# Decoder kernel: four of a head's 26 masked score pieces get their mask from VectorE instead of TensorE

## The chip, the cores and the metric

The kernel runs on one core of one Trainium2 chip. The metric is the device time of one execution in microseconds, as the median of several runs. TensorE does the matmuls (its weight loads have rows of their own, PEld), VectorE (DVE) and ScalarE (ACT) read and write both SBUF and PSUM, GpSimd (POOL) works in SBUF, and SyncE (SP) issues most DMAs.

## The reference

Two decoder layers run over 2048 tokens of width 256. Each has causal self-attention, cross-attention to a context of 1601 rows, and a feed-forward part. All attentions have 16 heads of 16 dimensions. The change touches only the cross-attention of the first layer, the one with an explicit mask:

```python
qh, kh, vh = (split_heads(qp), split_heads(kp), split_heads(vp))
scores = jnp.einsum('bhqd,bhkd->bhqk', qh, kh) / jnp.sqrt(jnp.float32(D_K))
scores = jnp.where(mask == 0, NEG_INF, scores)
attn = jax.nn.softmax(scores, axis=-1)
ctx = jnp.einsum('bhqk,bhkd->bhqd', attn, vh)
```

The mask has one value for each query and key (2048 x 1601), the same for all heads.

## The kernel before

All four attentions are one function, `attention_phase`; the flag `masked` is true only for the one that the change touches. A head's scores are computed twice.

**Units: the row maxima.** Softmax needs the maximum of every query row. A unit is 128 queries by 401 keys (or 398 at the end of a row): four matmuls on TensorE (line 548), then one instruction on VectorE that adds the mask in bfloat16 and takes the maximum (line 733, with a short row that reads the accumulator). A head has 16 x 4 = 64 units. Units go through three PSUM banks (`M_BANKS = 3`): TensorE fills unit g only after VectorE has finished unit g - 3, `pe.wait_ge(unit_used, g - M_BANKS + 1)`. `finish_max` (lines 745 to 758) turns a head's maxima into rows that are stacked under its queries, in five short VectorE steps that stand ahead of units 0 to 4 of the next head.

**Pieces: scores, mask, exponential, product.** Here the keys lie on the partitions. 13 tiles of up to 128 keys times two halves of 1024 queries make 26 pieces per head, numbered n = 0 to 25. The even pieces are the first halves. For a piece TensorE writes the scores (`scores`, line 569, eight matmuls, four column tiles in each of two PSUM banks), then adds the mask in PSUM (`mask_scores`, line 587, eight matmuls of -2^30 times the identity by a 0/1 mask in fp8, `mask_one`). ScalarE takes the exponential (line 475). After an odd piece, TensorE multiplies the tile by the values (`product`, line 609). Pieces use two PSUM buffers of two banks in turn, so the scores of piece n + 2 wait until the exponential of piece n is done.

**The order on TensorE** is written out by one loop, head by head and slot by slot. In slot n come: the scores of piece n + 2; the first units that are due here (the larger half of them); the mask products of piece n + 2; the product of the tile if n is odd; the other units. Each slot has two or three units, taken from the next head (slots 0 to 17, units 19 to 63) or from the head after that (slots 18 to 25, units 0 to 18). Slots 0|1 have 2 + 1 | 1 + 1 units (ahead of the mask products + behind them), slots 6|7 and 12|13 have 1 + 1 | 2 + 1, and slots 18|19 have 1 + 1 | 1 + 1.

**The order on VectorE** is simply unit after unit, head after head. Behind the last head's `finish_max` stand `scale(0)`, a copy, `invert(1)`, `scale(1)` and `invert_last`, which divide the heads' outputs by the sums of their exponentials (lines 789, 858, 784, 796). `invert(1)` and `scale(1)` have two DMAs between them, over which the inverse sums go to memory and come back (lines 302 and 309, on SP).

## Time and profile before

| what | value |
|---|---|
| runs (3) | 3050.74, 3052.56, 3059.14 us; median 3052.56 |
| profiled execution | 3052.74 us, of which the span is 3051.0 us |
| TensorE, busy share of the span | 92% |
| VectorE, busy share | 71% |
| ScalarE, busy share | 60% |
| mean granted TensorE clock | 0.952 of full speed |
| masked attention, from its first unit to its last unit on VectorE | 603.4 to 1269.5 us |
| its mask products on TensorE (line 587) | 3264 matmuls, from 645.8 to 1310.5 us |

A timeline row gives the start in the span, the time that the row took, the engine, the line, the operation with its tiles, a count, and in brackets how long the engine had stood idle and what released it. Matmuls are pipelined, so rows of TensorE overlap: four column tiles run at once, and a row of eight 512-column matmuls that lasts 0.62 us can have the next row start 0.44 us after it. The start-to-start distance is what to read.

### The profile page before, as it was taken

How to read it: one execution, taken by the hardware profiler on the slowest of the kernel's cores; microseconds unless marked ns; L12 is line 12 of the kernel's file. 1: busy time of each engine (PE TensorE's matmuls, PEld its weight loads, DVE VectorE, ACT ScalarE, POOL GpSimd, SP SyncE). 2: the span in 40 equal slices, each digit the busy share in tenths (PEclk: the TensorE clock that was granted, in tenths of full speed). 3: DMA queues.
4: the chain of work that ended last, by engine and by line, in shares of the span. 5: the costliest groups of instructions: out<-in, count | busy, mean ns of one | idle time of the engine just before them, and what ended most of it. 6: DMA issues, size and time to landing. Idle time of an engine off the chain costs nothing. (4 is left out here: it accounts for less than half of the span.)

```text
span 3051.0 us, 93944 instructions
## 1 busy us (share of the span) xinstructions
PE 2817.6 (92%) x39186; PEld 1046.2 (34%) x39187; DVE 2171.2 (71%) x6062; ACT 1824.3 (60%) x2158; POOL 542.7 (18%) x760
## 2 busy tenths in 40 slices
PE   4999999999999999967999998999999999899997
PEld 2522222522222222233222224652222222256664
DVE  7688986587878887565899993158888888652114
ACT  2388878436666666734588886234777777831222
POOL 0188870110000000001222113111000000002330
PEclk7899999979999999978899999997999999999999
DMA  3345541301110001102111112020111111111112
GB/s 98 111 130 131 135 111 35 118 18 25 25 26 25 17 24 26 36 20 76 33 47 43 42 45 83 1 74 23 39 52 52 52 53 32 35 58 62 44 43 86
DMA packets 120407, 166.79 MB, mean 55 GB/s; under 512 B 38227, under 2 KB 89310, under 8 KB 119984
## 3 DMA queue, kind: packets, MB, share of 16 engines
q1 hardware_dynamic: 102192, 117.21, 14.3%
q0 software_dynamic: 12320, 43.02, 4.6%
q8 instruction: 310, 5.08, 0.7%
q10 hardware_dynamic: 5472, 0.56, 0.2%
q14 instruction: 113, 0.93, 0.1%
HBM read 126.51 MB, written 26.72 MB: 50 GB/s over the span
## 5 line engine op out<-in xcount | busy, mean ns | idle before, releaser
L737 DVE TENSOR_REDUCE mpart<-ps 128x1 f32<-128x512 f32 (+2 forms) x1792 | 1014.2, 616 | 149.2 <-PE ps L548 148.1
L548 PE MATMUL ps<-stack 48*32 48x401 f16 (+5 forms) x13312 | 987.9, 355 | 55.3 <-DVE mpart L737 25.3
L475 ACT ACTIVATE xT<-ps,exp_scale 128x1024 f32<-128x1024 f32 (+3 forms) x800 | 794.6, 1028 | 284.6 <-PE ps L569 137.5
L475 ACT ACTIVATE cn<-ps,exp_scale 128x1024 f32<-128x1024 f32 (+4 forms) x800 | 743.1, 959 | 233.6 <-PE ps L569 119.7
L569 PE MATMUL ps<-stack 50*32 50x512 f16 (+3 forms) x11648 | 744.4, 377 | 56.2 <-ACT xT L475 42.3
L548 PEld LDWEIGHTS ps<-stack 48*32 48x32 f16 x13312 | 293.3, 91 | 1056.6 <-DVE mpart L737 562.8
L733 DVE CUSTOM_DVE_ANT_0 scrap<-ps,arena 128x401 bf16<-128x401 f32 (+1 forms) x1024 | 534.3, 574 | 128.0 <-PE ps L548 128.0
L609 PE MATMUL ps<-xT,vall 128*17 128x512 f32 (+4 forms) x3648 | 422.5, 524 | 2.2 <-POOL xT L434 1.4
L609 PE MATMUL ps<-cn,vall 128*17 128x512 f32 (+3 forms) x3392 | 412.9, 508 | 1.0 <-ACT cn L475 1.0
L569 PEld LDWEIGHTS ps<-stack 50*32 50x32 f16 x11648 | 194.6, 91 | 209.2 <-ACT xT L475 110.5
L727 DVE CUSTOM_DVE_ANT_0 scrap<-ps,scrap 128x128 bf16<-128x128 f32 (+3 forms) x512 | 247.6, 485 | 19.7 <-PE ps L548 15.1
L587 PE MATMUL ps<-arena,big 128*32 128x512 fp8e4 (+1 forms) x3264 | 256.8, 386 | 0.0
L1671 PE MATMUL ps<-arena,vall 128*128 x312 | 146.7, 593 | 0.6 <-ACT vall L1745 0.6
L1928 DVE TENSOR_TENSOR vall<-osb,ps 128x512 f32<-128x512 f32 x39 | 26.8, 688 | 146.0 <-PE ps L1671 146.0
L1761 ACT ACTIVATE osb<-ps 128x512 f32<-128x512 f32 x39 | 23.3, 597 | 169.8 <-PE ps L1671 169.8
L1152 POOL PARTITION_ALL_REDUCE small<-small x1 | 0.4, 371 | 687.4 <-issue 687.4
L609 PEld LDWEIGHTS ps<-xT,vall 128*17 128x17 f32 (+1 forms) x3648 | 71.5, 96 | 111.2 <-issue 46.1
L1574 POOL IOTA vall<- 128x16 f32 x1 | 0.2, 153 | 608.1 <-POOLq L248 608.1
L609 PEld LDWEIGHTS ps<-cn,vall 128*17 128x17 f32 (+1 forms) x3392 | 70.5, 96 | 109.0 <-issue 54.6
L422 POOL TENSOR_SCALAR arena<-wbuf 128x401 bf16<-128x401 int32 x64 | 101.2, 1581 | 6.3 <-DMA wbuf<-in_mask 2.5
L587 PEld LDWEIGHTS ps<-arena,big 128*32 128x32 bf16 (+1 forms) x3264 | 50.3, 94 | 120.8 <-issue 120.8
L733 DVE DVE_READ_ACCUMULATOR2_ANT mpart<- 128x1 f32 x1024 | 84.7, 83 | 0.0
(281 smaller groups left out, 2510.9 us busy)
## 6 DMA issues: line engine op xcount, KB each, us to landing
stack<-q_parts SPq DMA_DIRECT2D x384, 64.0 KB, 2.6
stack<-k_parts SPq DMA_DIRECT2D x192, 64.0 KB, 2.9
wbuf<-in_maskT POOLq DMA_DIRECT2D x24, 512.0 KB, 4.7
arena<-in_moe_w SPq DMA_DIRECT2D x19, 512.0 KB, 4.4
stack<-k_parts SPq DMA_DIRECT2D x192, 50.0 KB, 2.3
stack<-sums_inverse SPq DMA_DIRECT2D x16, 512.0 KB, 5.6
parts<-osb SPq DMA_DIRECT2D x240, 32.0 KB
wbuf<-in_mask POOLq DMA_DIRECT2D x16, 401.0 KB, 4.0
```

The source lines that it names most:

```text
L422: chain.link(nc.gpsimd.tensor_scalar(e.mask_add[:, t, a:a + n], stage.bitcast(I32), 0.0, MASKED, ALU.is_equal, ALU.mult))
L475: nc.scalar.activation(e.prob[tile % P_SLOTS][0:rows, half * HALF + first:(half + 1) * HALF], S_PS(g)[0:rows, first:HALF], ACT.Exp, scale= ...
L548: last = nc.tensor.matmul(bank[quarter(j), 0:w], qs[b][rows, t * P + 32 * j:t * P + 32 * j + 32], ks[b][rows, a:a + w], start=True, stop=True)
L569: last = nc.tensor.matmul(S_PS(g)[quarter(j), lo:hi], ks[b][at:at + KM, kt * P + 32 * j:kt * P + 32 * j + 32], qs[b][at:at + KM, half * HA ...
L587: last = nc.tensor.matmul(S_PS(g)[quarter(j), lo:hi], e.big16[0:rows, quarter(j)], e.mask_one[0:rows, kt, half * HALF + lo:half * HALF + h ...
L609: last = nc.tensor.matmul(O_PS[quarter(j, HD + 1), b0 * P:CH], e.values[0:rows, kt, h, :], weights[0:rows, b0:4, j, :], start=(kt == 0), s ...
L727: nc.vector.tensor_tensor_reduce(out=e.scrap[:, t % 3, 0:w], in0=src, in1=e.scrap[:, 3, CH - w:CH], scale=1.0, scalar=-3.0e38, op0=ALU.add ...
L733: nc.vector.tensor_tensor_reduce(out=e.scrap[:, g % 4, 0:w], in0=src, in1=e.mask_add[:, t, a:a + w], scale=1.0, scalar=-3.0e38, op0=ALU.ad ...
L737: nc.vector.tensor_reduce(dst, src, AX, ALU.max).then_inc(unit_used, 1)
L1671: last = nc.tensor.matmul(bank, e.pair_xT[i % 2][:, c, :], w, start=(c == 0), stop=(c == NC - 1))
L1761: nc.scalar.activation(e.gated_s[i % 2], a_bank(i), ACT.Silu).then_inc(pair_silu, 1)
L1928: nc.vector.tensor_tensor(e.pair_h[i % 2], e.gated_s[i % 2], b_bank(i), ALU.mult).then_inc(pair_h, 1)
```

## The change

For pieces 2, 8, 14 and 20 of each head, `mask_scores` returns at once, and `scores` counts up a new semaphore, `scored`. VectorE waits for it and does the masking itself: one `scalar_tensor_tensor` over 128 x 1024 elements that reads the scores in PSUM and the fp8 mask in SBUF and writes the sum back to the same PSUM. ScalarE's exponential of such a piece waits for this instruction (`piece_masked`). Waits on `s_ready` are counted in 22 pieces per head instead of 26. All pieces concerned are even ones with full 128-key tiles. On VectorE the instruction for piece n stands directly ahead of the first unit of slot n - 2. The last pieces, for which no unit is left (piece 20 of head 14 and all four of head 15), stand together behind the last `finish_max`, ahead of `scale(0)`.

```diff
+        by_dve = (2, 8, 14, 20) if masked else ()
+        own = [n for n in range(ns) if n not in by_dve]
+        scored, piece_masked = (sem("scored"), sem("piece_masked")) if masked else (None, None)
...
-                        act.wait_ge(s_ready, g + 1)
+                        if n in by_dve:
+                            act.wait_ge(piece_masked, h * len(by_dve) + by_dve.index(n) + 1)
+                        else:
+                            act.wait_ge(s_ready, h * len(own) + own.index(n) + 1)
...
-                    if not masked:
+                    if n in by_dve:
+                        last.then_inc(scored, 1)
+                    elif not masked:
                         last.then_inc(s_ready, 1)
...
                     kt, rows, half, first, diagonal, _ = slots[n]
+                    if n in by_dve:
+                        return
...
+                def mask_piece(h, i):
+
+                    n = by_dve[i]
+                    kt, rows, half, _, _, _ = slots[n]
+                    dve.wait_ge(scored, h * len(by_dve) + i + 1)
+                    nc.vector.scalar_tensor_tensor(out=S_PS(h * ns + n)[0:rows], in0=e.mask_one[0:rows, kt, half * HALF:(half + 1) * HALF],
+                                                   scalar=MASKED, in1=S_PS(h * ns + n)[0:rows], op0=ALU.mult, op1=ALU.add).then_inc(piece_masked, 1)
+
+                def unit_of_step(h, u):
+
+                    for i, n in enumerate(by_dve):
+                        ahead = 1 if n - 2 <= turn else 2
+                        if h - ahead >= 0 and before[n - 2] == u:
+                            mask_piece(h - ahead, i)
+                    unit(h, u)
...
-                        unit(h, u)
+                        unit_of_step(h, u)
...
                 for step in range(MAX_STEPS):
                     finish_max(H - 1, step)
+                for h in range(H - 2, H):
+                    for i, n in enumerate(by_dve):
+                        if h + (1 if n - 2 <= turn else 2) >= H:
+                            mask_piece(h, i)
                 scale(0)
```

How the rows move. First TensorE, slots 6 and 7 of head 0. L569 (L575 in the changed file) are scores, L548 (L554) units, four matmuls each, L587 (L597) mask products, L609 (L619) the product. Before:

```order
L569 MATMUL ps<-stack_13216 32x512 x8
L548 MATMUL ps<-stack_13216 32x401 x4
L587 MATMUL ps<-arena,big 32x512 x8
L548 MATMUL ps<-stack_13216 32x398 x4
L569 MATMUL ps<-stack_13216 32x512 x8
L548 MATMUL ps<-stack_13216 32x401 x8
L587 MATMUL ps<-arena,big 32x512 x8
L609 MATMUL ps<-cn,vall 17x512 x4
```

And now:

```order
L575 MATMUL ps<-stack_13216 32x512 x8
L554 MATMUL ps<-stack_13216 32x401 x4
L554 MATMUL ps<-stack_13216 32x398 x4
L575 MATMUL ps<-stack_13216 32x512 x8
L554 MATMUL ps<-stack_13216 32x401 x8
L597 MATMUL ps<-arena,big 32x512 x8
L619 MATMUL ps<-cn,vall 17x512 x4
```

The mask products of piece 8, between the two units of slot 6, are gone. Everything else keeps its order.

VectorE at the same place. The rows named ISA are units of L733 (now L743), each followed by the row that reads its accumulator; the rows begin with the last unit of slot 5. Before:

```order
L733 ISA scrap,mpart<-ps,arena 128x401
L733 ISA mpart 128x1
L733 ISA scrap,mpart<-ps,arena 128x401
L733 ISA mpart 128x1
L733 ISA scrap,mpart<-ps,arena 128x398
```

And now:

```order
L743 ISA scrap,mpart<-ps,arena 128x401
L743 ISA mpart 128x1
L754 SCALAR_TENSOR_TENSOR ps<-arena,ps 128x1024
L743 ISA scrap,mpart<-ps,arena 128x401
L743 ISA mpart 128x1
L743 ISA scrap,mpart<-ps,arena 128x398
```

The masking of piece 8 stands between the last unit of slot 5 and the first of slot 6.

VectorE at the end of the attention, behind the last unit of head 15 (L789 are `scale(0)` and `scale(1)`, L784 is `invert(1)`). Before:

```order
L745 TENSOR_REDUCE mfin<-mpart 128x16
L749 TENSOR_SCALAR mrest<-mfin 128x16
L751 TENSOR_SCALAR mneg<-mrest 128x16
L753 SCALAR_TENSOR_TENSOR mneg<-mneg,mrest 128x16
L758 STREAM_TRANSPOSE mturn<-mneg 128x32
L789 TENSOR_TENSOR parts<-parts,stack_13216 128x1024 x2
L858 COPY parts<-ident 128x128
L784 RECIPROCAL parts<-parts 128x128
L789 TENSOR_TENSOR parts<-parts,stack_13216 128x1024 x2
```

And now:

```order
L784 STREAM_TRANSPOSE mturn<-mneg 128x32
L754 SCALAR_TENSOR_TENSOR ps<-arena,ps 128x1024 x5
L815 TENSOR_TENSOR parts<-parts,stack_13216 128x1024 x2
L888 COPY parts<-ident 128x128
L810 RECIPROCAL parts<-parts 128x128
L815 TENSOR_TENSOR parts<-parts,stack_13216 128x1024 x2
```

Five maskings (head 14's piece 20 and head 15's four) stand ahead of `scale(0)` and `invert(1)`.

## Rows read from the trace of the kernel before

**Rows 1.** Windows: a stretch of the masked attention (columns as named)

```profile
core 0: us, PE busy (x) PEld busy (x) DVE busy (x) ACT busy (x) POOL busy (x), PEclk, DMA share, GB/s
900.00:1000.00 100.00, 99.30 (x1816) 26.83 (x1808) 79.60 (x313) 69.43 (x65) 0.00 (x0) 1.00 0.11 27
```

**Rows 2.** Timeline of slots 6 and 7 of a middle head

```profile
1038.04 0.56 PE L569 MATMUL ps<-stack 50*32 50x512 f16 x8
1038.43 0.58 DVE L733 CUSTOM_DVE_ANT_0 scrap<-ps,arena 128x401 bf16<-128x401 f32 x1 [0.66 <-PE ps L548]
1038.54 0.62 PE L587 MATMUL ps<-arena,big 128*32 128x512 fp8e4 x8
1038.93 0.57 DVE L733 CUSTOM_DVE_ANT_0 scrap<-ps,arena 128x401 bf16<-128x401 f32 x1
1039.08 0.35 PE L548 MATMUL ps<-stack 48*32 48x398 f16 x4
1039.43 0.08 DVE L733 DVE_READ_ACCUMULATOR2_ANT mpart<- 128x1 f32 x1
1039.57 0.10 PEld L548 LDWEIGHTS ps<-stack 48*32 48x32 f16 x4 [0.35 <-DVE mpart L733]
1039.85 0.62 PE L587 MATMUL ps<-arena,big 128*32 128x512 fp8e4 x8
```

**Rows 3.** Timeline of slots 0 and 1 of the same head

```profile
1028.79 0.57 DVE L733 CUSTOM_DVE_ANT_0 scrap<-ps,arena 128x398 bf16<-128x398 f32 x1
1029.68 0.41 PE L569 MATMUL ps<-stack 50*32 50x512 f16 x8 [0.23 <-ACT xT L475]
1029.91 0.34 PE L548 MATMUL ps<-stack 48*32 48x401 f16 x4
```

**Rows 4.** Timeline of slots 18 and 19, where a head's units end

```profile
1016.16 0.22 DVE L745 TENSOR_REDUCE mfin<-mpart 128x16 f32<-128x64 f32 x1
1016.30 0.57 DVE L733 CUSTOM_DVE_ANT_0 scrap<-ps,arena 128x401 bf16<-128x401 f32 x1
1016.33 2.17 ACT L475 ACTIVATE cn<-ps,exp_scale 128x1024 f32<-128x1024 f32 x2 [0.80 <-PE ps L587]
1018.13 0.55 PE L569 MATMUL ps<-stack 50*32 50x512 f16 x8
```

**Rows 5.** Lines by form, VectorE: what 1024, 512 and 2048 elements take

```profile
L1033 DVE SCALAR_TENSOR_TENSOR wbuf<-vall,wbuf 128x1024 f32<-128x1024 f32 x1 | 1.2, 1226 | 0.0
L714 DVE SCALAR_TENSOR_TENSOR parts<-ps,bcol,parts 128x512 f16<-128x512 f32 x44 | 33.0, 751 | 54.2 <-ACT parts L455 54.2
L1068 DVE TENSOR_TENSOR turning<-ps,vall 128x2048 f32<-128x2048 f32 x4 | 9.2, 2292 | 0.1
```

**Rows 6.** Timeline of the end: heads 14 and 15, then the division

```profile
1269.77 2.12 ACT L475 ACTIVATE xT<-ps,exp_scale 128x1024 f32<-128x1024 f32 x2 [0.78 <-PE ps L587]
1270.64 2.32 DVE L789 TENSOR_TENSOR parts<-parts,stack 128x1024 f32<-128x1024 f32 x2
1271.39 0.41 PE L569 MATMUL ps<-stack 50*32 50x512 f16 x8
1286.44 0.95 DVE L784 RECIPROCAL parts<-parts 128x128 f32<-128x128 f32 x1 [13.35 <-DMA parts<-sums]
1296.65 2.36 DVE L789 TENSOR_TENSOR parts<-parts,stack 128x1024 f32<-128x1024 f32 x2 [9.26 <-DMA stack<-sums_inverse]
1303.82 0.41 PE L569 MATMUL ps<-stack 50*32 50x512 f16 x8
1316.10 0.96 DVE L796 RECIPROCAL osb<-ps 128x128 f32<-128x128 f32 x1 [17.08 <-PE ps L685]
```

**Rows 7.** The unmasked cross-attention: a window, then three starts of `finish_max`

```profile
2200.00:2210.00 10.00, 9.30 (x124) 1.76 (x116) 6.42 (x13) 5.96 (x7) 0.00 (x0) 0.66 0.27 64
...
2188.21 0.22 DVE L745 TENSOR_REDUCE mfin<-mpart 128x16 f32<-128x64 f32 x1
2226.92 0.22 DVE L745 TENSOR_REDUCE mfin<-mpart 128x16 f32<-128x64 f32 x1
2263.28 0.22 DVE L745 TENSOR_REDUCE mfin<-mpart 128x16 f32<-128x64 f32 x1
```

More of the change, by code:

```diff
@@ L256, in load @@
                     if h >= 3:
-                        sp.wait_ge(s_ready, (h - 2) * ns)
+                        sp.wait_ge(s_ready, (h - 2) * len(own))
                     for row, (k_part, q_part) in zip(range(0, KQ, HD), ((0, 0), (0, 1), (1, 0))):
@@ L305, in load_inverse @@
                     sp.wait_ge(rec_out, 16 * (c + 1))
-                    sp.wait_ge(s_ready, (14 + c) * ns)
+                    sp.wait_ge(s_ready, (14 + c) * len(own))
                     for a in range(0, S, HALF):
@@ L570, in scores @@
                                                     qs[b][at:at + KM, half * HALF + lo:half * HALF + hi],
-                                                    start=True, stop=not (crossed or masked))
+                                                    start=True, stop=not (crossed or masked and n not in by_dve))
                         if crossed:
```

## The prediction, made before the changed kernel was run

> **What bounds the kernel now.** I read the page's busy shares and the 40 slices first: the masked attention is the stretch where TensorE is fullest. A window says it exactly: in 100 us TensorE is busy for 99.3, VectorE for 79.6, ScalarE for 69.4, at a granted clock of 1.00 [rows 1]. So TensorE is the bound, and shares alone would welcome the change: it takes work from the full engine and gives it to one that is idle a fifth of the time.
>
> Shares don't say when the idle time comes, so I read the timeline of two slots [rows 2]. VectorE's idle time is one piece, 0.66 us, in front of the unit that TensorE fills right behind the product. During mask products and product TensorE fills no unit, and VectorE runs dry. Elsewhere the two are tied: the second unit of slot 7 (weights at 1039.57, 0.35 idle, released by VectorE) starts as soon as the bank that it needs is read. That bank held the first unit of slot 6, whose VectorE row starts at 1038.93 and whose accumulator row ends at 1039.43 + 0.08 = 1039.51; 0.06 later TensorE goes on. The mask products of piece 9 follow at 1039.85, and the product behind them.
>
> **What the change removes.** A group of mask products (8 matmuls) starts at 1038.54 and the next unit at 1039.08 [rows 2]: 0.54 us. There are 4 x 16 = 64 such groups, so at most 64 x 0.54 = 34.6 us.
>
> **What it adds.** 64 instructions on VectorE. The trace has none that reads and writes PSUM, or that reads fp8. Nearest: the same operation with an immediate scalar on 1024 fp32 elements in SBUF, 1.226 us; with a PSUM input, 512 elements take 0.751. From 512 to 2048 elements it costs (2.292 - 0.751)/1536 = 1.00 ns each, so 1024 with PSUM come to 0.751 + 0.51 = 1.26 [rows 5]. What counts behind it is the distance to the next start, which I call P. Two 1024-element rows together take 2.32 us [rows 6], so the second starts about 1.10 after the first; a unit of 0.58 has its follower 0.50 later [rows 2]. I take P = 1.14, with ends at 1.10 and 1.29 (nothing overlapped, some slack). The duration, for ScalarE's start, is 1.22 to 1.29.
>
> A page states another distance. The Trainium skill, VectorE: DVE Perf Modes, "The DRAIN you can't avoid", says that "the next op does not start until the 8-stage pipe empties", though the section behind it lets an instruction that isn't held start earlier. The rows of this trace agree with the second, by the overlaps just named. By the first the sum below would be some 7 us higher.
>
> **Pieces 8 and 14 (slots 6|7, 12|13).** VectorE takes its instructions in order: last unit of slot 5, masking, first unit of slot 6. The scores are there in time (from 1038.04, for 0.56, while the unit ahead lasts until 1038.93) [rows 2]. The masking starts at 1038.93, the first unit of slot 6 P later, its bank is free P later, and the second unit of slot 7 starts at 1039.57 + P. TensorE is in order too: piece 9's mask products and the product stand behind that unit. The 0.54 saved lies ahead of this wait and is swallowed by it. Before, TensorE waited there already, so the whole of P is paid: 1.14. Then come mask products and product without a new unit; VectorE, which ran dry there for 0.66 us before, works off its full banks and is dry again when the next unit comes, so the next pair of slots runs at the old pace. Nothing is given back, since nothing else there has slack. ScalarE ends the late exponential 1.1 us after the masking, well ahead of the scores two slots on.
>
> **Piece 2 (slots 0|1).** Here TensorE before stood waiting for ScalarE (1029.68), and the first unit of slot 1 starts at 1029.91 [rows 3]. Slot 0's first unit, on VectorE at 1028.79, now starts P later, at 1029.93, and frees its bank at 1029.93 + 0.50 + 0.08 + 0.06 = 1030.57. Cost 0.66, that is P - 0.48.
>
> **Piece 20 (slots 18|19).** The unit that needs the late bank stands behind the product, so there the units cost nothing. But ScalarE is late: the masking follows `mfin` at 1016.30 and is ready by 1017.55, the exponential that began at 1016.33 runs from 1017.6 to 1018.7, and the scores two slots on, at 1018.13 before, wait for it until 1018.8 [rows 4]. A further 0.1 goes to the units behind. Cost 0.75.
>
> Pieces 2, 8 and 14 occur so in heads 0 to 14: 15 x (0.66 + 2 x 1.14) = 44.1 us. Piece 20 in heads 0 to 13: 14 x 0.75 = 10.5.
>
> **The end.** Head 14's piece 20 is masked behind the five steps, from 1270.6 (where `scale(0)` stood) to 1271.9; its exponential and the next end near 1273.1 and 1274.1, and the scores that started at 1271.39 wait: 1.8 us. Head 15 has no units. A piece's own chain (scores 0.41, masking 1.25, exponential 1.06) is longer than the slots by about 0.5: 4 x 0.5 = 2.0. Then the division. Piece 20's scores came at 1303.82, so its masking ends near 1305.5, and behind it stand `scale(0)` 2.3, the copy 0.2 and the reciprocal 0.95: 1309.0 instead of 1287.4. From there to `scale(1)` it is two DMAs on SP's queue, 9.26 us, then 2.36: 1320.6. `invert_last` began at 1316.10 and needs VectorE [rows 6]. TensorE's totals and the last head's DMAs wait for it: 4.5 us.
>
> **Sum.** 44.1 + 10.5 + 1.8 + 2.0 + 4.5 = 62.9. On the profiled execution (3052.74, span 3051.0 and 1.7 around it) that gives 3115.6; the median of the runs is 0.2 lower, 3115.5. I say 3116. With P = 1.10 the 45 terms with P are 1.8 us less, with 1.29 they are 6.8 more, and the end may be off by 3 either way: 3111 to 3126 for this case. Edits that cost nothing: the counts of `s_ready` (the pieces that SP and the stacks wait for are masked by TensorE as before), and the five steps of `finish_max`, up to 0.9 us later, whose rows reach the stack over a microsecond ahead of the first scores that read them, which are late by as much.
>
> **Rivals.**
>
> *The clock falls as well.* Each stall leaves TensorE idle for about 1.2 us, and for a little more just ahead of it. In the unmasked attention, which has no mask products, the granted clock falls in some heads: 0.66 of full speed between 2200 and 2210, that is partly at 1.2 GHz. A head with such a fall takes 2226.92 - 2188.21 = 38.71 us, one without 2263.28 - 2226.92 = 36.36: 2.35 us more [rows 7]. Against it: the second of these heads has no fall, and in the masked stretch the clock stands at 1.00 [rows 1]. One fall per head gives 16 x 2.35 = 38, so 3153. The Trainium skill, TensorE: Matmul & The Clock Gate, "A second HAM failure mode: psum-queue depth-cycling", tells of the same mechanism: short idle times between groups of matmuls that cycle through banks make the clock oscillate. Chance 0.23.
>
> *The saved products count after all.* If the units behind a masking are not tied as tightly as rows 2 show, and TensorE takes its 0.54 off each wait, pieces 8 and 14 cost 0.60 and piece 2 0.12: 15 x 1.32 = 20, with the other terms (18.8) 39, so 3092. Against it: the wait at 1039.57 has no slack. Chance 0.10.
>
> *The masking is dear.* In place in PSUM, with fp8, it might take twice the time, as no row excludes: P = 2.3, 45 x 1.16 = 52 more, and piece 20 and the end 20 more: 3188. Chance 0.06.
>
> *VectorE absorbs it: faster.* Three pairs of slots hold 3 x 0.66 = 2.0 us of VectorE's idle time, more than P, and a masking comes only every three or four pairs. If TensorE weren't held at the second unit behind a masking, it would keep most of 34.6 us and lose only the 8 at the end: 3052.6 - 34.6 + 8 = 3026. It decides at the unit of 1039.57: its bank would have to be free more than 1.14 us ahead of TensorE's wish, and by rows 2 it is just free. Chance 0.04, with 0.02 that gain and loss cancel to within 0.3% (about 9 us, which is what a measurement of this kernel tells from no change).
>
> **How the numbers follow.** The case of the sum has 0.55. Faster 0.04, same 0.02, slower 0.94. The range reaches from the third case's side, 3090, to one fall of the clock in each head and a little more, 3160; outside are the dear masking and the gain.
>
> **What would show it.** The new rows: 64, of 1.2 to 1.3 us, each followed by a unit about 1.14 later; mask products 2752 instead of 3264. In slots 7 and 13 TensorE's weights for the second unit should stand idle for about 1.5 us, released by VectorE, and heads should lie 3.7 us farther apart. VectorE's share in the masked stretch should rise, TensorE's fall to some 90%. In the end `scale(1)` should come just ahead of `invert_last`. The forecast is wrong if the second unit of slots 7 and 13 doesn't wait, or if the clock leaves 1.00 in the masked stretch.

## The result, and the profile after

The changed kernel takes 3131.97 us (median of 4 runs, 3129.27 to 3134.27) against 3055.85 (4 runs, 3050.74 to 3060.33): a ratio of 1.0249, with a 95% interval of 1.0227 to 1.0271. It is slower, by 76 us. The forecast was 3116, with a range of 3090 to 3160.

The window that answers to [rows 1], with the columns of that group:

```profile
900.00:1000.00 100.00, 89.84 (x1582) 24.64 (x1575) 82.10 (x294) 62.80 (x58) 0.00 (x0) 0.98 0.08 20
```

TensorE went from 99.3 to 89.8 busy, by more than the mask products that it gave up (nine groups of 0.54 at most in such a stretch), and VectorE rose only to 82.1. No engine is full now. The granted clock is 0.98 where it was 1.00.

The timeline of slots 6 and 7, which answers to [rows 2]:

```profile
1079.15 0.35 PE L554 MATMUL ps<-stack 48*32 48x401 f16 x4
1080.06 1.23 DVE L754 SCALAR_TENSOR_TENSOR ps<-arena,ps 128x1024 f32<-128x1024 fp8e4 x1
1080.20 0.35 PE L554 MATMUL ps<-stack 48*32 48x401 f16 x4
1081.19 0.57 DVE L743 CUSTOM_DVE_ANT_0 scrap<-ps,arena 128x401 bf16<-128x401 f32 x1
1081.82 0.10 PEld L554 LDWEIGHTS ps<-stack 48*32 48x32 f16 x4 [1.53 <-DVE mpart L743]
1081.83 0.35 PE L554 MATMUL ps<-stack 48*32 48x401 f16 x4 [1.28 <-DVE mpart L743]
1082.11 0.61 PE L597 MATMUL ps<-arena,big 128*32 128x512 fp8e4 x8
1082.55 1.63 PE L619 MATMUL ps<-xT,vall 128*17 128x512 f32 x8
```

The masking starts at 1080.06 and the next unit 1.13 later. TensorE has issued the first unit of slot 7 (1080.20) and its second one stands until 1081.82, released by VectorE; matmuls are idle for 1.28. From the last unit of slot 5, which opens the pair here (1079.15), to the mask products of piece 9 (1082.11) are 2.96 us; before they were 1.83 (1038.02 below to 1039.85 in [rows 2]). The last row shows a fall of the clock: eight matmuls of the product last 1.63 us instead of 1.03.

How much each pair of slots pays is read from the starts of the product's weights, one set in each odd slot, in the weight loads of the timeline. The kernel before (its row of L548 is the last unit of slot 5, just ahead of slots 6 and 7):

```profile
1016.94 0.32 PEld L609 LDWEIGHTS ps<-xT,vall 128*17 128x17 f32 x8
1020.25 0.32 PEld L609 LDWEIGHTS ps<-cn,vall 128*17 128x17 f32 x8
...
1026.71 0.33 PEld L609 LDWEIGHTS ps<-xT,vall 65*17 65x17 f32 x8
1030.41 0.32 PEld L609 LDWEIGHTS ps<-xT,vall 128*17 128x17 f32 x8
1033.63 0.32 PEld L609 LDWEIGHTS ps<-cn,vall 128*17 128x17 f32 x8
...
1038.02 0.10 PEld L548 LDWEIGHTS ps<-stack 48*32 48x32 f16 x4 [0.85 <-DVE mpart L733]
...
1056.19 0.32 PEld L609 LDWEIGHTS ps<-xT,vall 128*17 128x17 f32 x8
1059.16 0.33 PEld L609 LDWEIGHTS ps<-cn,vall 128*17 128x17 f32 x8
```

The changed kernel:

```profile
1010.81 0.32 PEld L619 LDWEIGHTS ps<-xT,vall 128*17 128x17 f32 x8
1015.00 0.32 PEld L619 LDWEIGHTS ps<-xT,vall 128*17 128x17 f32 x8
...
1021.45 0.33 PEld L619 LDWEIGHTS ps<-cn,vall 65*17 65x17 f32 x8
1025.80 0.32 PEld L619 LDWEIGHTS ps<-xT,vall 128*17 128x17 f32 x8
1029.02 0.32 PEld L619 LDWEIGHTS ps<-xT,vall 128*17 128x17 f32 x8
1032.24 0.32 PEld L619 LDWEIGHTS ps<-cn,vall 128*17 128x17 f32 x8
1036.60 0.32 PEld L619 LDWEIGHTS ps<-cn,vall 128*17 128x17 f32 x8
...
1053.83 0.32 PEld L619 LDWEIGHTS ps<-xT,vall 128*17 128x17 f32 x8
1056.56 0.32 PEld L619 LDWEIGHTS ps<-xT,vall 128*17 128x17 f32 x8
```

A pair without a masking takes 3.22 (1025.80 to 1029.02), as before (1030.41 to 1033.63). The pair with piece 8 takes 4.36 (1032.24 to 1036.60), 1.14 more, and piece 14's 4.35, 1.13 more. Piece 2's pair takes 4.35 (1021.45 to 1025.80) against 3.70, 0.65 more. Piece 20 first gains 0.24 (2.73 instead of 2.97 in the last pair shown), then loses 0.88 (1010.81 to 1015.00 is 4.19 instead of 3.31): 0.64. Together 3.56 per head.

The first steps of `finish_max` show the whole head, three of fifteen:

```profile
1010.28 0.22 DVE L771 TENSOR_REDUCE mfin<-mpart 128x16 f32<-128x64 f32 x1
1056.03 0.22 DVE L771 TENSOR_REDUCE mfin<-mpart 128x16 f32<-128x64 f32 x1
1103.21 0.22 DVE L771 TENSOR_REDUCE mfin<-mpart 128x16 f32<-128x64 f32 x1
```

The head between the first two takes 45.75, 3.5 more than the 42.21 of before; the next takes 47.18, and so do nine more of the fourteen. They hold one fall of the clock each, at 1.44 us. An eleventh lies in head 0: the second of the sixteen first steps comes 4.39 us later than before (682.85 against 678.46), and 2.92 of this are maskings.

Slots 18 and 19, answering to [rows 4], and then the end, answering to [rows 6]:

```profile
1056.16 1.22 DVE L754 SCALAR_TENSOR_TENSOR ps<-arena,ps 128x1024 f32<-128x1024 fp8e4 x1
1057.41 2.12 ACT L481 ACTIVATE cn<-ps,exp_scale 128x1024 f32<-128x1024 f32 x2 [2.03 <-DVE ps L754]
1058.58 0.41 PE L575 MATMUL ps<-stack 50*32 50x512 f16 x8 [0.31 <-ACT cn L481]
...
1378.19 1.23 DVE L754 SCALAR_TENSOR_TENSOR ps<-arena,ps 128x1024 f32<-128x1024 fp8e4 x1 [7.06 <-PE ps L575]
1379.33 2.35 DVE L815 TENSOR_TENSOR parts<-parts,stack 128x1024 f32<-128x1024 f32 x2
1391.11 2.36 DVE L815 TENSOR_TENSOR parts<-parts,stack 128x1024 f32<-128x1024 f32 x2 [8.43 <-DMA stack<-sums_inverse]
1393.38 0.95 DVE L822 RECIPROCAL osb<-ps 128x128 f32<-128x128 f32 x1
...
1395.88 0.58 SPq L248 DMA_DIRECT2D parts<-osb  x1
```

The masking of the last head's piece 20 is followed by the whole division, and `scale(1)` at 1391.11 stands just ahead of `invert_last` (1393.38), where before it had been done for 17 us. From the last head's first step (1337.91) to the `place_last` transfers (1395.88) it is 57.97 us; before it was 48.97.

Not all of these 9.0 us are the maskings' own. The window of this stretch in the changed kernel, and the same stretch of e5, an experiment below with the same five maskings:

```profile
1337.91:1395.88 57.97, 51.28 (x602) 15.20 (x594) 14.96 (x21) 36.79 (x36) 0.00 (x0) 0.94 0.09 25
```

```profile
1339.48:1394.50 55.02, 50.27 (x638) 15.47 (x634) 14.96 (x21) 36.62 (x36) 0.00 (x0) 1.00 0.10 26
```

The changed kernel has two more falls of the clock here (the windows 1342.30 to 1345.70 and 1352.50 to 1355.90 stand at 0.50 of full speed, 1.2 GHz), behind stalls in which TensorE waits for ScalarE. Where the end has no fall it takes 55.02 (e5) or 55.06 (e10, below), 6.1 more than before. So 6.1 are maskings and 2.9 are falls, and between the first of the first steps and `place_last` this trace holds thirteen falls.

From those transfers to the end of the span, both kernels take the same (1732.3 and 1732.4 us). The whole difference of the spans, 77.2, lies in the masked attention:

| term | measured, us | forecast |
|---|---|---|
| pieces 2, 8, 14: 15 heads x 2.92 | 43.8 | 44.1 |
| piece 20: 14 heads x 0.61 to 0.64 | 8.6 | 10.5 |
| the end, without its falls | 6.1 | 8.3 |
| 13 falls of the clock: 11 x 1.44, and 2.9 in the end | 18.7 | 0 |

### The profile page after: what moved, and what is told of

Read it like the earlier page. It is cut to its first block and busy times, and to the rows that moved or that the text cites. A ratio compares the mean times of both kernels' runs of the same rounds, so it can differ in the third digit from the quotient of the medians.

```text
span 3128.2 us, 92985 instructions
## 1 busy us (share of the span) xinstructions
PE 2828.4 (90%) x38675; PEld 1051.8 (34%) x38675; DVE 2239.6 (72%) x6126; ACT 1825.0 (58%) x2158; POOL 545.8 (17%) x760
## 5 line engine op out<-in xcount | busy, mean ns | idle before, releaser
L554 PE MATMUL ps<-stack 48*32 48x401 f16 (+5 forms) x13312 | 994.2, 356 | 109.8 <-DVE mpart L743 49.9
L575 PE MATMUL ps<-stack 50*32 50x512 f16 (+3 forms) x11648 | 739.6, 379 | 68.6 <-ACT xT L481 48.5
L554 PEld LDWEIGHTS ps<-stack 48*32 48x32 f16 x13312 | 295.7, 91 | 1124.9 <-DVE mpart L747 562.2
L743 DVE CUSTOM_DVE_ANT_0 scrap<-ps,arena 128x401 bf16<-128x401 f32 (+1 forms) x1024 | 534.9, 573 | 130.7 <-PE ps L554 130.7
L619 PE MATMUL ps<-xT,vall 128*17 128x512 f32 (+4 forms) x3648 | 427.9, 530 | 2.6 <-POOL xT L437 1.8
L619 PE MATMUL ps<-cn,vall 128*17 128x512 f32 (+3 forms) x3392 | 414.2, 510 | 1.1 <-ACT cn L481 1.0
L575 PEld LDWEIGHTS ps<-stack 50*32 50x32 f16 x11648 | 194.2, 90 | 234.3 <-ACT xT L481 120.3
L597 PE MATMUL ps<-arena,big 128*32 128x512 fp8e4 (+1 forms) x2752 | 222.8, 395 | 0.0
L619 PEld LDWEIGHTS ps<-xT,vall 128*17 128x17 f32 (+1 forms) x3648 | 71.5, 96 | 111.0 <-issue 47.8
L619 PEld LDWEIGHTS ps<-cn,vall 128*17 128x17 f32 (+1 forms) x3392 | 70.4, 96 | 108.8 <-issue 55.4
L754 DVE SCALAR_TENSOR_TENSOR ps<-arena,ps 128x1024 f32<-128x1024 fp8e4 x64 | 78.3, 1223 | 37.0 <-PE ps L575 37.0
L743 DVE DVE_READ_ACCUMULATOR2_ANT mpart<- 128x1 f32 x1024 | 84.2, 82 | 0.0
```

Of the source, the lines that this page charges most:

```text
L554: last = nc.tensor.matmul(bank[quarter(j), 0:w], qs[b][rows, t * P + 32 * j:t * P + 32 * j + 32], ks[b][rows, a:a + w], start=True, stop=True)
L575: last = nc.tensor.matmul(S_PS(g)[quarter(j), lo:hi], ks[b][at:at + KM, kt * P + 32 * j:kt * P + 32 * j + 32], qs[b][at:at + KM, half * HA ...
L597: last = nc.tensor.matmul(S_PS(g)[quarter(j), lo:hi], e.big16[0:rows, quarter(j)], e.mask_one[0:rows, kt, half * HALF + lo:half * HALF + h ...
L619: last = nc.tensor.matmul(O_PS[quarter(j, HD + 1), b0 * P:CH], e.values[0:rows, kt, h, :], weights[0:rows, b0:4, j, :], start=(kt == 0), s ...
L743: nc.vector.tensor_tensor_reduce(out=e.scrap[:, g % 4, 0:w], in0=src, in1=e.mask_add[:, t, a:a + w], scale=1.0, scalar=-3.0e38, op0=ALU.ad ...
L754: nc.vector.scalar_tensor_tensor(out=S_PS(h * ns + n)[0:rows], in0=e.mask_one[0:rows, kt, half * HALF:(half + 1) * HALF], scalar=MASKED, i ...
```

## The experiments

The table gives all twelve. "Head" is the distance of first steps without a fall of the clock, "falls" the number of the 14 distances that are longer by 1.4 us or more (in the changed kernel this leaves out the fall in head 0 and the two in the end; in e7 two of the distances hold two falls), "end" the time from the last head's first step to `place_last`. The ratio is to the kernel before.

| run | head, us | falls | end, us | median, us | ratio, 95% interval |
|---|---|---|---|---|---|
| before | 42.21 | 0 | 48.97 | 3052.26 to 3055.85 | |
| changed | 45.75 | 10 | 57.97 | 3131.97 | 1.0227 to 1.0271 |
| e1 products left out only | 41.95 | 0 | 48.96 | 3050.53 | 0.9975 to 1.0005 |
| e2 VectorE's work only | 45.75 | 0 | 48.97 | 3105.17 | 1.0153 to 1.0187 |
| e3 odd pieces | 43.73 | 0 | 54.81 | 3081.65 | 1.0071 to 1.0105 |
| e4 piece 8 only | 43.34 | 9 | 49.38 | 3086.64 | 1.0088 to 1.0122 |
| e5 filled | 45.74 | 10 | 55.02 | 3131.42 | 1.0238 to 1.0277 |
| e6 other order in slots 7, 13 | 44.24 | 1 | 56.34 | 3095.86 | 1.0119 to 1.0155 |
| e7 end on TensorE | 45.74 | 11 | 48.98 | 3120.65 | 1.0191 to 1.0229 |
| e9 pieces 8, 14, 20 | 45.09 | 6 | 56.87 | 3116.13 | 1.0186 to 1.0216 |
| e10 the same, filled | 45.09 | 0 | 55.06 | 3100.54 | 1.0137 to 1.0166 |
| e8 320 columns of 9 odd pieces | 41.19 | 0 | 49.01 | 3040.67 | 0.9933 to 0.9964 |
| e11 384 columns | 41.13 | 0 | 49.11 | 3035.11 | 0.9932 to 0.9961 |
| e12 480 columns | 41.31 | 0 | 49.14 | 3037.48 | 0.9928 to 0.9957 |

### The saving without the work, and the work without the saving

e1 leaves the four pieces unmasked:

```diff
                 def mask_piece(h, i):
 
                     n = by_dve[i]
                     kt, rows, half, _, _, _ = slots[n]
-                    dve.wait_ge(scored, h * len(by_dve) + i + 1)
+                    return
...
-                            act.wait_ge(piece_masked, h * len(by_dve) + by_dve.index(n) + 1)
+                            act.wait_ge(scored, h * len(by_dve) + by_dve.index(n) + 1)
```

> The changed kernel with the 64 VectorE instructions left out and nothing in their place: pieces 2, 8, 14 and 20 of each head get no mask at all (ScalarE waits for their scores alone). TensorE so does 64 x 0.54 = 34.6 us less than in the kernel before, and VectorE no more. Theory A (the second unit of slots 7 and 13 is tied to VectorE's read, so whatever TensorE saves ahead of it is swallowed): nothing at pieces 8 and 14, at most 0.5 per head at pieces 2 and 20, so 3048 to 3056 us, and in the trace the weights of that second unit stand idle for about 0.9 us, released by VectorE (0.35 before). Rival B (TensorE is the bound and what it saves counts): 3056 - 34.6 = 3021 us.

Measured: 3050.53, no difference from before. 34.6 us of matmuls are gone and nothing comes of it. The timeline of its slots 6 and 7 shows why:

```profile
1035.60 0.35 PE L554 MATMUL ps<-stack 48*32 48x401 f16 x4
...
1036.64 0.10 PEld L554 LDWEIGHTS ps<-stack 48*32 48x32 f16 x4 [0.50 <-DVE mpart L743]
1037.13 0.10 PEld L554 LDWEIGHTS ps<-stack 48*32 48x32 f16 x4 [0.40 <-DVE mpart L743]
1037.41 0.12 PEld L597 LDWEIGHTS ps<-arena,big 128*32 128x32 bf16 x8 [0.18 <-issue]
```

Both units of slot 7 wait for VectorE, which paces them. From the opening unit to piece 9's mask products it is 1.81 us (1035.60 to 1037.41), with 0.54 less to do than before, when it was 1.83. The weights stood for 0.40 to 0.50, not for 0.9: the waiting time was spread over two units. Only piece 20's saving of 0.25 stays, the 0.26 by which a head is shorter.

e2 keeps all mask products and gives VectorE the same instruction, from and to SBUF, at the same places:

```diff
+                    dve.wait_ge(spared, len(added_so_far) + 1)
+                    added_so_far.append(n)
+                    nc.vector.scalar_tensor_tensor(out=e.scrap[0:rows, 3, :].bitcast(FP8), in0=e.mask_one[0:rows, kt, half * HALF:(half + 1) * HALF],
+                                                   scalar=0.0, in1=e.vall[0:rows, 0:4, :].rearrange("p t c -> p (t c)"), op0=ALU.mult, op1=ALU.add, saturate=False).then_inc(spared, 1)
...
-                        unit(h, u)
+                        unit_of_step(h, u)
```

The instruction's result goes to the fourth quarter of `scrap`, so the units take turns in three quarters instead of four.

> The kernel before, with all its mask products, and on VectorE the same instruction form (fp8 mask, fp32 second operand, 128x1024) at the places of pieces 2, 8, 14 and 20, but from and to SBUF, with nobody waiting for its result; none behind the last head's steps, 59 in all. Theory A (the stall is VectorE's time ahead of a tied bank, the saved products are swallowed): heads become longer by 0.66 + 2 x 1.14 = 2.9 us (44 in all, piece 20's 0.75 was ScalarE's wait and goes, the end too), and the clock falls as in the changed kernel (about 1.4 us in each of 11 or 12 heads): 3055 + 44 + 16 = 3115 us. Rival B (the changed kernel was longer by VectorE's work less the products saved): it would be slower than the changed kernel less its end and its ScalarE wait: 3132 - 20 + 34.6 = 3147 us.

Measured: 3105.17, heads 45.75 apart, exactly as in the changed kernel without a fall. So what a head pays is VectorE's time, and the saved products count for nothing: shown from both sides. Two points of the expectation fell. The clock never fell, though the pairs with maskings took 4.36 as in the changed kernel. And piece 20 costs the same 0.63 although ScalarE waits for nobody:

```profile
1043.44 1.21 DVE L750 SCALAR_TENSOR_TENSOR scrap<-arena,vall 128x1024 fp8e4<-128x1024 fp8e4 x1
...
1046.35 0.35 PE L551 MATMUL ps<-stack 48*32 48x401 f16 x4 [0.22 <-DVE mpart L736]
```

Behind the steps of `finish_max` VectorE has its units and the steps to do with no idle time between, so the units there are tied as well.

### One slot later

e3 changes one line:

```diff
-        by_dve = (2, 8, 14, 20) if masked else ()
+        by_dve = (3, 9, 15, 21) if masked else ()
```

> Pieces 3, 9, 15 and 21 are masked by VectorE instead of 2, 8, 14 and 20: the same work on both engines, one slot later, so that the masking stands ahead of the first unit of the slot that ends in the product. Then VectorE's idle time of 0.66 us behind that slot takes part of it, and TensorE's saved 0.54 lies behind the tied unit. Theory A (the place costs, not the work): a piece costs 1.14 - 0.66 = about 0.5, in 15 heads x 4 pieces 28, the end 8 as before, stalls too short for the clock to fall: 3055 + 36 = 3091 us, 3080 to 3100. Rival (the cost is that of 64 instructions wherever they stand): 3132 us, as the changed kernel. Rival C (ScalarE becomes late, since the exponential of an odd piece has less time before the scores two slots on): over 3132.

Measured: 3081.65. The same 64 instructions cost 1.52 per head instead of 3.54. By the starts of the product's weights, read as above, piece 9's two pairs take 3.00 and 3.89 instead of twice 3.22, 0.45 more, piece 15's 0.47, piece 21's 0.63, and piece 3's nothing (6.91 instead of 6.92). The clock stays at 1.00 in all heads. The place makes more than half of the price.

e6 leaves the pieces as they are, but lets TensorE issue one unit instead of two ahead of the product in slots 7 and 13:

```diff
-                        middle = -(-len(now) // 2)
+                        middle = 1 if masked and n in (7, 13) else -(-len(now) // 2)
```

> The changed kernel, but in slots 7 and 13 TensorE issues one unit instead of two ahead of mask products and product, and two behind it. So the unit that has to wait for VectorE's late read is behind the product, and nothing is held up. Theory A (TensorE's order turns VectorE's lateness into a stall): pieces 8 and 14 cost about 1.14 - 0.66 = 0.5 each instead of 1.14, since VectorE no longer runs dry behind the masking; heads 44.4 to 44.5 us apart instead of 45.75, fewer clock falls; the end as in the changed kernel: 3055 + 15 x 2.25 + 9 = 3098 us without falls, 3112 with as many as before. Rival (the cost is VectorE's time, and order doesn't matter): 3132.

Measured: 3095.86, 36 us back by the order of a few matmuls, with the same work on every engine: 15 x 1.51 = 23 from shorter heads, and in the profiled executions eleven falls fewer (one in the heads and one in the end instead of thirteen), about 16. That adds up to 39; the 3 us too many are within what runs of one kernel differ. TensorE now does mask products and product while VectorE masks:

```profile
1009.47 1.22 DVE L754 SCALAR_TENSOR_TENSOR ps<-arena,ps 128x1024 f32<-128x1024 fp8e4 x1
1009.89 0.61 PE L597 MATMUL ps<-arena,big 128*32 128x512 fp8e4 x8
1010.33 1.03 PE L619 MATMUL ps<-cn,vall 128*17 128x512 f32 x8
```

Neither engine stands still until the product ends. Pieces 8 and 14 cost (44.24 - 42.21 - 0.65 - 0.64)/2 = 0.37 each.

### One piece, and the clock

e4 is the same line with `by_dve = (8,)`.

> VectorE masks piece 8 alone, TensorE the other 25. Theory A: one stall of P = 1.14 us in each of 15 heads, 17 us, half a microsecond in the last head, nothing at the division, since that masking comes before the middle of the last head: 3055 + 17.6 = 3073 us if a single stall per head leaves the clock alone. Theory D (any stall of this size makes the clock fall): 1.4 more per head, 3094 us. If pieces add up only by their number, a quarter of the changed kernel's +77: 3075, with heads of 42.21 + 1.24; by theory A alone heads lie 43.35 us apart, 1.14 more than the kernel before's 42.21.

Measured: 3086.64. Heads without a fall are 43.34 apart, 1.13 more, which is P to a hundredth. Nine of the fourteen hold a fall and are 1.5 longer. So both theories were half right: one stall of 1.28 us per head is enough for the clock to fall, in most heads but not in all.

In e2 pieces 2, 8 and 14 make the pairs just as long, and the clock never fell. What differs is the mask products, and with them the length of the stall: where they are kept they fill part of the gap, and TensorE's matmuls stand for 1.04 (piece 8) and 1.01 us (piece 14) in e2, against 1.28 in the changed kernel. e5 puts as many matmuls in their place, with zero weights, added to the output bank (the zero weights lie in the fourth quarter of `scrap`, so the units use three):

```diff
                     if n in by_dve:
+                        if n > 2:
+                            for bank in range(2):
+                                for j in range(-(-rows // 32)):
+                                    at = half * HALF + bank * CH
+                                    nc.tensor.matmul(O_PS[quarter(j, HD + 1), 0:CH], e.scrap[0:rows, 3, 0:HD + 1],
+                                                     e.mask_one[0:rows, kt, at:at + CH], start=False, stop=False)
                         return
```

> The changed kernel, and in the place of the mask products that it left out TensorE does as many of the same width with zero weights (pieces 8, 14 and 20; piece 2 not), added to the output bank, so that nothing is changed by them. The other three kernels of this kind so far: products kept beside the stalls (heads all 45.75 us apart, no clock fall) and products gone (47.2 in 10 of 14 heads). Theory E (the clock falls because TensorE does less around a stall, since 8 groups of matmuls are gone ahead of it): with this filling the falls go or become few, heads lie 45.75 apart, and the kernel with 1.5 us of work more per head is faster than the changed kernel: 3132 - 15 = 3117 us. Rival F (the stall alone makes the clock fall): as the changed kernel, 3132, or slower by up to 48 x 0.54 = 26 us if the filling isn't swallowed.

Measured: 3131.42, as the changed kernel, with falls still there. 48 groups more make no head longer (45.74), which shows once more that they are swallowed. By its time alone theory E fell. The profiled execution has ten falls instead of thirteen, but the clock also stands at half speed for longer at the opening of the attention (until 656.1 us instead of 649.4), which makes the first distance about 2.9 us longer; e7 shows the same without any filling. The windows show more: where the falls are now. First e5, whose head begins at 729.40, then the changed kernel, whose head begins at 728.59 (piece 2's stall comes 13 us into the head, piece 8's 25):

```profile
740.00:745.00 5.00, 3.84 (x76) 1.15 (x68) 4.34 (x14) 3.67 (x4) 0.00 (x0) 0.98 0.34 99
745.00:750.00 5.00, 5.00 (x72) 1.18 (x68) 3.02 (x13) 2.07 (x3) 0.00 (x0) 0.67 0.19 42
...
755.00:760.00 5.00, 3.96 (x84) 1.01 (x80) 4.34 (x16) 2.59 (x3) 0.00 (x0) 1.00 0.01 3
```

```profile
750.00:755.00 5.00, 3.64 (x76) 1.21 (x68) 4.34 (x14) 3.18 (x3) 0.00 (x0) 1.00 0.00 0
755.00:760.00 5.00, 5.00 (x72) 1.01 (x67) 2.77 (x11) 2.23 (x3) 0.00 (x0) 0.66 0.01 3
```

In e5 the clock falls behind piece 2's stall, the one without filling, and holds at 1.00 behind piece 8's, where TensorE was idle for 1.04 of 5 us instead of 1.36. The expectation of e10 below calls the filled stalls "as long"; they are not, they last 1.04 and 1.01 instead of 1.28. All ten falls of that trace lie 15 to 16 us into their head, behind piece 2. So e9 and e10 leave piece 2 to TensorE, `by_dve = (8, 14, 20)`, e9 without the filling, e10 with it.

> The changed kernel with piece 2 masked by TensorE again; VectorE masks 8, 14 and 20. Heads without a clock fall: 42.21 + 2 x 1.13 + 0.64 = 45.1 us apart. Theory E (the clock falls behind a stall where mask products were left out) and rival F (the stall alone does it) both give falls of 1.4 to 1.5 us in many heads: 3055 + 15 x 2.9 + 8 for the end + about 14 for ten falls = 3120 us; without falls 3107.

> The run before this one, and in the place of the left-out mask products of pieces 8, 14 and 20 TensorE does as many of the same width with zero weights, added to the output bank. In the first kernel with this filling every fall that was left came behind piece 2's stall, the one without filling, though the stalls of 8 and 14 were as long. Theory E: no falls at all here, all heads 45.1 us apart, 3107 us, some 14 below its neighbour, with more work on TensorE. Rival F (the stall alone): falls as in its neighbour, the same time. Rival G (the falls move to another place in the head): heads 46.5 us apart in most cases, the same time.

Measured: 3116.13 and 3100.54. The heads without a fall are the same, 45.09, and e10 has no fall in any head nor in the end. More matmuls, less time. The windows at the same stall (piece 14's), e9 first:

```profile
715.00:720.00 5.00, 3.64 (x60) 0.90 (x53) 3.69 (x11) 2.47 (x3) 0.00 (x0) 0.86 0.01 2
```

```profile
710.00:715.00 5.00, 3.99 (x68) 0.83 (x60) 4.22 (x15) 2.88 (x3) 0.00 (x0) 1.00 0.01 2
```

And e10's second unit at that stall, which in e9 stands for 1.28:

```profile
713.39 0.35 PE L555 MATMUL ps<-stack 48*32 48x401 f16 x4 [1.01 <-DVE mpart L752]
```

So filling the gap takes these falls away. It does so in two ways at once, more work ahead of the stall and a shorter stall, and no run takes the two apart. Nor does the length of a stall decide alone: in the end of e5 stalls of 1.59 and 1.39 us are followed by no fall, while the same wait of 1.39 for ScalarE is followed by one in the end of the changed kernel and of e1 (where VectorE masks nothing), and by none in e6. Behind piece 2, TensorE is idle for 0.30, 0.41 and 0.45 us in e5 as in e6, and the clock falls there in ten of fourteen heads of e5 and in one of e6. What singles out a head or a stall stays open.

Of the 15.6 us between the medians the two profiled executions explain 10.5 by the clock: six falls in the heads (8.7) and one in the end (1.8). They differ by another 4.1 ahead of the attention's first unit and by 5 behind its end, where the kernels are the same; that is what runs differ by, and not the filling.

### The end

e7 gives the five maskings that have no unit behind them back to TensorE:

```diff
+        def dve_masks(h, n):
+            return n in by_dve and h + (1 if n - 2 <= turn else 2) < H
...
-                    if n in by_dve:
+                    if dve_masks(h, n):
                         return
...
-                for h in range(H - 2, H):
-                    for i, n in enumerate(by_dve):
-                        if h + (1 if n - 2 <= turn else 2) >= H:
-                            mask_piece(h, i)
```

> The changed kernel, but the five maskings that stood behind the last head's steps (piece 20 of head 14, pieces 2, 8, 14 and 20 of head 15) are TensorE's products again. The time from the last head's first step to the place_last transfers was 48.97 us before and 57.97 after. Theory: the 9.0 us are the last head's longer chain (1.8 + 2.0) and the division behind the maskings (4.5); all of it goes back to 49, so 3132 - 9 = 3123 us. Rival (the end is late because the last exponentials are): less than 4 us come back.

Measured: 3120.65, and the end takes 48.98, as before, at a clock of 1.00. All of the 9.0 comes back, the 6.1 of the maskings and the 2.9 of the two falls, and the difference of medians, 11.3, is near it. The expectation added the 9.0 up as 1.8 + 2.0 + 4.5, without the falls. The heads keep theirs: the profiled execution has thirteen in eleven of the fourteen distances (two distances are 48.63), and at 3129.14 it is the slowest of this kernel's four.

### A version that uses VectorE's idle time

The runs say where the change could pay: VectorE is idle only behind the product's slot (0.66 us per pair), and a saving of TensorE counts only there. e8 starts from the kernel before; VectorE masks the last 320 columns of pieces 3, 5, ... 19 of heads 0 to 14, behind TensorE's mask products for the others:

```diff
+        by_dve, WIDE = tuple(range(3, 20, 2)) if masked else (), 320
...
-                        lo, hi = bank * CH, (bank + 1) * CH
+                        lo, hi = bank * CH, (bank + 1) * CH - (WIDE if bank and dve_masks(h, n) else 0)
...
+                    dve.wait_ge(s_ready, h * ns + n + 1)
+                    part = S_PS(h * ns + n)[0:rows, HALF - WIDE:]
+                    nc.vector.scalar_tensor_tensor(out=part, in0=e.mask_one[0:rows, kt, (half + 1) * HALF - WIDE:(half + 1) * HALF],
+                                                   scalar=MASKED, in1=part, op0=ALU.mult, op1=ALU.add).then_inc(piece_masked, 1)
...
+                    for i, n in enumerate(by_dve):
+                        if before[n - 2] + 1 == u:
+                            mask_part(h - 1, i)
                     unit(h, u)
```

> The kernel before, with VectorE masking the last 320 of the 1024 columns of pieces 3, 5, ... 19 of heads 0 to 14, each ahead of the second unit of the slot two ahead (which ends in the product), and TensorE the other 704. VectorE's part is some 0.1 + 0.32 = 0.43 us and fits its idle time of 0.66; TensorE saves 4 x 320 of its columns, 0.17 us, behind the tied unit, where the removal isn't swallowed. Theory A (idle time of VectorE is only to be had behind the product, and savings of TensorE only count there): eight or nine pairs of slots per head go from 3.22 to about 3.06 us, 15 x 8.5 x 0.16 = 20 us, so 3032 us, faster than both kernels. Rival (ScalarE or the second unit's bank ties the pair, and savings vanish as in the run with products left out): 3053. Rival (the masking delays as in the changed kernel): 9 x 0.43 x 15 = 58 us more, 3110.

e11 and e12 set `WIDE` to 384 and 480.

> As the kernel with 320 columns on VectorE, with 384. There a pair of slots took 3.09 us (TensorE 99.5% busy, VectorE 91%), and one masking 0.41 to the next start. With 384 it takes 0.47: VectorE needs 2.57 + 0.47 = 3.04 per pair, TensorE about 3.22 - 0.16 = 3.06. So TensorE is still the bound by a little, heads 41.0 us apart instead of 41.19, 3 us less in all: 3037. Rival (ScalarE's start, which waits for the masking, becomes the tie): heads over 41.2.

> The same with 480 columns: VectorE would need 2.57 + 0.57 = 3.14 us per pair, TensorE 3.03. Theory A (beyond about 390 columns VectorE's idle time is used up and it paces the pair): pairs of 3.14, heads 42.21 - 9 x 0.08 = 41.5, 3044 us, slower than with 384 columns and still a little faster than the kernel before. Rival (what TensorE saves goes on counting): heads 40.7, 3032.

Measured: 3040.67, 3035.11 and 3037.48, all three faster than the kernel before by 0.5%, and not to be told from each other by their intervals. The window of e11 and VectorE's rows of e12:

```profile
900.00:1000.00 100.00, 99.25 (x1877) 27.83 (x1876) 92.61 (x346) 71.41 (x67) 0.00 (x0) 1.00 0.10 24
```

```profile
1033.05 0.66 DVE L753 SCALAR_TENSOR_TENSOR ps<-arena,ps 128x480 f32<-128x480 fp8e4 x1
1033.62 0.57 DVE L741 CUSTOM_DVE_ANT_0 scrap<-ps,arena 128x401 bf16<-128x401 f32 x1
...
1036.12 0.66 DVE L753 SCALAR_TENSOR_TENSOR ps<-arena,ps 128x480 f32<-128x480 fp8e4 x1
```

A pair takes 3.09 us with 320 columns, 3.06 with 384 and 3.07 with 480 (1033.05 to 1036.12). With 480, VectorE never runs dry in these pairs: masking 0.57 and five units of 0.50. The expectation of 3.14 counted the units at 2.57 in all, 0.07 too much. So up to 384 columns TensorE is the bound, from there VectorE. With 320 columns a pair gained 0.13 instead of 0.16 and a head 1.02 instead of 1.36, which makes 15 x 0.34 = 5 of the 9 us by which e8 fell short of its 3032; the rest is within what its runs differ (3033.37 to 3044.86).

## Why the prediction was right, and what was missing

The time, 3131.97, lies in the stated range of 3090 to 3160, but outside the 3111 to 3126 of the case that the sum describes. The range held it because it had been stretched for a fall of the clock. By the forecast's own sign (it is wrong "if the clock leaves 1.00 in the masked stretch") its main case fell on this point, while the direction, the tied bank and the price per masking held.

*Nature of the bound.* Right. Slots 6 and 7 behave as [rows 2] said: the second unit of slot 7 stands 1.53 us, released by VectorE, and the pair is longer by 1.14 and 1.13, the P of the forecast.

*The saved products.* Right, and now shown: leaving them out gains nothing (e1), keeping them costs nothing (e2), and filling their place costs nothing (e5). The rival that they count after all is excluded, and so are the ones by which VectorE absorbs the maskings or the instruction is dear (64 rows of 1.223 us).

*P.* 1.14 was taken, 1.13 measured, with a duration of 1.22. The Trainium skill, VectorE: DVE Perf Modes, "The DRAIN you can't avoid", has the next operation wait until the pipe is empty, and adds that one that is not held starts earlier. The unit behind a masking starts 0.09 to 0.10 before the masking's row ends (1080.06 + 1.23 against 1081.19): these rows agree with the addition and not with the first statement, as the prediction had it.

*Piece 2.* 0.66 forecast, 0.65 measured.

*Piece 20.* 0.75 forecast, 0.64 measured: a loss of 0.88 less a gain of 0.24 that the forecast hadn't. Its mechanism was only half right. ScalarE's wait is there (0.31 at 1058.58), but "the unit that needs the late bank stands behind the product, so there the units cost nothing" was wrong: e2, without ScalarE's wait, loses as much through the units. The two delays lie side by side.

*The end.* 8.3 forecast, 9.0 measured, and removed by e7. That the two agree is luck: 2.9 of the 9.0 are two falls of the clock, and what the forecast meant comes to 6.1. Its two parts, the delay of the last pieces and the division, were each too high by about 1.1. In e5, whose end has no fall, the last masking starts 37.26 us behind the last head's first step, where the scores before were ready at 34.60: 2.7 of delay instead of 1.8 + 2.0. From there to `invert_last` it is 15.26 instead of 11.87, 3.4 more instead of 4.5, mostly because the two DMAs took 8.5 instead of the 9.26 of before.

*The clock.* The step that failed is the one that left it at 1.00 in the likeliest case. The rival with a chance of 0.23 had the mechanism, and overstated its size: 38 us, for a fall in all of 16 heads at the 2.35 of [rows 7]. It was 13 falls worth 18.7 us. The fall that it took from the unmasked attention was a longer one: there the clock stands at 0.50 from 2202.30 to 2209.10, here from 755.20 to 758.60. With 18.7 the main sum, 3115.6, comes to 3134.3; less what was too high in the end (2.2), at piece 20 (1.9) and at the other pieces (0.3), that is 3129.9, against 3130.0 of the profiled execution. The Trainium skill, TensorE: Matmul & The Clock Gate, "A second HAM failure mode: psum-queue depth-cycling", tells of such oscillation from short idle times between groups of matmuls; this trace agrees in so far as every fall in the heads and in the end follows a stall. That a stall alone doesn't settle it is shown by the end of e5, where stalls of 1.59 and 1.39 us are followed by none.

## What to carry to other kernels

Before work is moved off a full engine, find in the timeline the instruction that ends each wait: a saving ahead of an instruction that is tied to another engine's progress is worth nothing, and a saving behind it may count for most of its size (in e8 0.13 of 0.17 us per pair). Put the moved work where the other engine runs dry, no wider than that idle time, and look at what is queued behind the instruction that will wait; moving one unit behind the product gave back 36 of 76 us. In an in-order queue with three banks between producer and consumer, shares of busy time say little: VectorE was idle a fifth of the time, and all of it lay in front of one unit in five.

## What was not expected of the hardware

- The granted clock fell in nine of fourteen heads with one stall of TensorE of 1.28 us (e4) and in six of fourteen with two (e9), where the mask products ahead of the stall were gone. It fell in none where they or as many zero matmuls stood in their place (e2, e10): the pairs of slots were equally long, and the stalls 1.04 and 1.01 us. Filling the gap saved seven falls, 10.5 us, in one profiled execution against another. A fall cost 1.44 us here (1.50 in e4), and a longer one 2.35 in the unmasked attention.
- `scalar_tensor_tensor` in place in PSUM with an fp8 operand takes as long as between SBUF operands: 1.223 us against 1.219 for 1024 elements (e2). For 320, 384 and 480 elements it took 0.491, 0.557 and 0.657.
